# A four-block convolution kernel: strip semaphore, pointwise quarters, ScalarE's share and the last image's rows

## The reference

```python
x = x + _L0_conv_ref(_gn(x), W, pw, pb, cw, cb)          # kernels mixed per pixel
x = x + _L1_conv_ref(_gn(x), weights, tap_offsets)       # 9 taps at fractional offsets
x = x + _L2_conv_ref(_gn(x), gk1, gk2, w1, b1, ...)      # 4 gated experts, batch norm
x = x + _L3_conv_ref(_gn(x), w1, w2, alpha, bn...)       # two 3x3 convs, residual

# L0: para = conv3x3(relu(conv1x1(x, pw) + pb), cw) + cb            (16 coefficients per pixel)
#     t[o,e,p] = sum_j W[o,j,e] * patches3x3(x)[j,p];  out[o,p] = sum_e t[o,e,p] * para[e,p]
# L2, for each expert e: g = gate(x); y = relu(bn(conv3x3(g, w1[e]) + b1[e]))
#     out += relu(bn(conv3x3(y, w2[e]) + b2[e]) + x)
# L3: w1, w2 are sums of ten kernels weighted by alpha
#     out = relu(bn2(conv3x3(relu(bn1(conv3x3(x, w1))), w2)) + x)
```

## Time and profile before

| | us |
|---|---|
| median of 3 runs | 394.69 |
| lowest and highest | 394.27, 398.84 |
| profiled execution | 394.71 |
| its span | 392.8 |
| PE busy | 368.4 (94%) |
| DVE busy | 260.9 (66%) |
| POOL busy | 97.7 (25%) |
| ACT busy | 60.2 (15%) |

### The profile page before, as it was taken

The page is one execution under the profiler, slowest core; times in us unless marked ns, Lnnn a source line. Parts: engine busy times, 40 slices in busy tenths (PEclk is TensorE's granted clock), DMA queues, the critical chain, the costliest instruction groups (busy, mean ns, idle before and its releaser), DMA issues.

```text
span 392.8 us, 8970 instructions
## 1 busy us (share of the span) xinstructions
PE 368.4 (94%) x3446; PEld 261.1 (66%) x3446; DVE 260.9 (66%) x469; ACT 60.2 (15%) x129; POOL 97.7 (25%) x248
## 2 busy tenths in 40 slices
PE   4799999999999999999999999799999979799991
PEld 3557888888888888888888887323366742466670
DVE  4675777877878878878788788434425376902255
ACT  1125010010100100101001000420041029442200
POOL 4527777888600000000000000114010019400000
PEclk9999999999999999999999999889999989999998
DMA  7654847527357076173481000489600000000032
GB/s 225 167 138 121 202 119 194 153 53 199 98 127 200 23 187 160 47 199 101 117 204 26 0 0 0 105 183 217 126 2 3 2 1 2 0 3 5 3 108 110
DMA packets 28641, 38.59 MB, mean 98 GB/s; under 512 B 7072, under 2 KB 23776, under 8 KB 27936
## 3 DMA queue, kind: packets, MB, share of 16 engines
q1 hardware_dynamic: 18080, 27.52, 27.6%
q10 hardware_dynamic: 10528, 10.61, 10.4%
HBM read 4.56 MB, written 2.10 MB: 17 GB/s over the span
## 4 chain that ended last, share of the span: by engine, by line
PE 86%; DVE 7%; DMA 2%; ACTq 1%; issue 1%; ACT 1%; SPq 0%; POOL 0%; DVEq 0%; POOLq 0%
PE ps L866 23%; PE ps L867 23%; PE ps L870 8%; PE ps L917 8%; PE ps L1056 5%; PE ps L1040 5%; PE ps L901 4%; PE ps L985 3%; PE ps L1009 2%; DMA X<-in_x 2%; PE ps L841 2%; ACTq L374 1%; PE ps L1025 1%; PE ps L930 1%; PE ps L975 1%
## 5 line engine op out<-in xcount | busy, mean ns | idle before, releaser
L866 PE MATMUL ps<-WA,HS 128*128 128x512 f32 x384 | 153.6, 400 | 0.7 <-DVE TS L1121 0.7
L867 PE MATMUL ps<-WB,LS 128*128 128x512 f32 x384 | 150.7, 392 | 0.0
L1143 DVE TENSOR_TENSOR PROD<-ps,PT 128x512 f32<-128x512 f32 x128 | 88.4, 691 | 39.2 <-PE ps L870 33.4
L1127 DVE TENSOR_REDUCE RED<-PROD 128x32 f32<-128x512 f32 x128 | 86.4, 676 | 0.0
L866 PEld LDWEIGHTS ps<-WA,HS 128*128 128x128 f32 x384 | 72.4, 189 | 19.2 <-issue 0.9
L867 PEld LDWEIGHTS ps<-WB,LS 128*128 128x128 f32 x384 | 72.4, 189 | 14.9
L870 PE MATMUL ps<-WC,TS 96*128 96x512 f32 x128 | 50.6, 395 | 0.0
L482 POOL MEMSET IMG<- 128x67 f32 x1 | 0.2, 154 | 139.4 <-DVE X L1133 139.4
L901 PE MATMUL ps<-REPL,ONE 128*128 128x256 f32 x120 | 29.4, 398 | 1.7 <-DVE X L1328 1.3
L724 ACT ACTIVATE HS<-HS 32x40 fp32r<-32x40 f32 x21 | 5.7, 274 | 164.3 <-DMA TS<-LO 164.0
L917 PE MATMUL ps<-SK,WE 128*32 128x512 f32 x256 | 30.0, 628 | 0.0
(11 more groups left out here) (223 smaller groups left out, 335.0 us busy)
## 6 DMA issues: line engine op xcount, KB each, us to landing
LS<-HS SPq DMA_DIRECT2D x7, 960.0 KB, 5.8
HS<-HI SPq DMA_DIRECT2D x60, 80.0 KB, 2.5
SK<-IMG SPq DMA_DIRECT2D x32, 131.8 KB, 2.6
HS<-LO ACTq DMA_DIRECT2D x32, 80.0 KB, 2.7
LS<-LO ACTq DMA_DIRECT2D x32, 80.0 KB, 2.7
HS<-HI SPq DMA_DIRECT2D x30, 79.8 KB, 2.6
TS<-LO SPq DMA_DIRECT2D x34, 63.8 KB, 4.0
out_x<-OT SPq DMA_DIRECT2D x8, 256.0 KB, 2.1
```

What stands on the lines that cost most here:

```text
L866: pe.matmul(ps[b][:, :], px(HS, dy), WA[:, dy, :], start=(dy == 0), stop=False)
L867: pe.matmul(ps[b][:, :], px(LS, dy), WB[:, dy, :], start=False, stop=False)
L1127: ve.tensor_reduce(RED[j % 2][:, 32 * b:32 * b + 32], PROD[b % 2][:, :].rearrange("p (o e) -> p o e", e=E0), AX.X, ALU.add).then_inc(sum_d ...
L1143: ve.tensor_tensor(PROD[b % 2][:, :].rearrange("p (o e) -> p o e", e=E0), ps[b][:, :].rearrange("p (o e) -> p o e", e=E0), para.broadcast_ ...
```

## The change

- The eight DMAs of the first strip's lo rows signal a semaphore of their own, `first_lo`. VectorE waits for it after its first PT copy and clears the lo rows' column there; the wait for the remaining twelve DMAs and the clearing of TS stay behind the second copy. (The counts that later strips wait for are adapted.)
- The 1x1 convolution runs quarter 0 after three chunks and quarters 1 to 3 after all eight. One fill instead of two stands before the transposes.
- ScalarE writes hidden rows of images 1, 2 and 3, VectorE of image 0 and the constant rows; ten fills instead of thirteen.
- The sixteen raw z columns are copied by ScalarE, once VectorE has written the experts' means; ZE waits for them.
- The last image: VectorE writes rows 0 to 8 and then 9 to 14 of quarters 0 to 2; ScalarE rows 0 to 8 of quarter 3, row 15 of quarters 0 to 2, then rows 9 to 15 of quarter 3. The convolution's half h = 0 waits for the first parts and h = 1 for the last; two fills instead of four.

```diff
--- before.py
+++ after.py
@@ constants @@
-FIRST_REST = NREST - 5
+FIRST_REST = NREST - 13
-IMG_V = 40
...
+        def image_quarters(q0, q1, r0, r1):
+
+            return rows(IMG, 1, H).rearrange("p (q r) c -> p q r c", r=QR)[:, q0:q1, r0:r1, :]
+
+        def x_quarters(q0, q1, r0, r1):
+
+            return X[:, :].rearrange("p (q r c) -> p q r c", r=QR, c=W)[:, q0:q1, r0:r1, :]
...
-        def stack_lo(queue, s, half):
+        def stack_lo(queue, s, half, done):
...
-                                    LO[32 * b:32 * b + 32, :, bass.ds(s * (SL // 2) + g, S0)].bitcast(F32)).then_inc(strip_rest[half], 16)
+                                    LO[32 * b:32 * b + 32, :, bass.ds(s * (SL // 2) + g, S0)].bitcast(F32)).then_inc(done, 16)
...
@@ ScalarE @@
-            stack_lo(act, 0, 0)
+            stack_lo(act, 0, 0, first_lo)
...
-            for b in (1, 3):
+            for b in (1, 2, 3):
 
                 act.activation(hidden_rows(b, 1, 5), ps[b][:, 0:5 * W].rearrange("p (r c) -> p r c", c=W), ACT.Relu, bias=Q2[:, 7, 3:4],
                                scale=Q2[:, 7, 2:3]).then_inc(hidden_by_scalar, 1)
+            act.wait_ge(bn_input_ready, 2)
+            for e in range(NE):
+                for b in range(B):
+                    ins = act.activation(ZRAW[32 * e:32 * e + 32, b:b + 1], ps[e][32 * b:32 * b + 32, 6 * W + 1:6 * W + 2], ACT.Copy)
+                ins.then_inc(raw_z_done, 1)
             act.wait_ge(bn2_ready, 1)
...
             act.wait_ge(coef_ready, 3)
-            norm(rows(IMG, 1 + IMG_V, H - IMG_V), IMG_V, H).then_inc(image_by_scalar, 1)
+            for q0, q1, r0, r1 in ((3, 4, 0, CR + 1), (0, 3, QR - 1, QR), (3, 4, CR + 1, QR)):
+                act.activation(image_quarters(q0, q1, r0, r1), x_quarters(q0, q1, r0, r1), ACT.Identity, bias=NMR[:, 0:1],
+                               scale=RS[:, 0:1]).then_inc(image_by_scalar, 1)
             act.wait_ge(w3_mixed, 1)
-            act.wait_ge(image_by_vector, 3)
-            act.wait_ge(image_by_scalar, 3)
+            act.wait_ge(image_by_vector, 4)
+            act.wait_ge(image_by_scalar, 5)
             act.activation(X[:, :], X[:, :], ACT.Identity, bias=S3[:, 3:4]).then_inc(x3_shifted, 1)
...
@@ TensorE @@
-            for pair in range(2):
-                pe.wait_ge(norm0_done, 5 if pair == 0 else NCH)
-                tiles = [(b, j) for j in (2 * pair, 2 * pair + 1) for b in range(B)]
+            for chunks, quarters in ((3, (0,)), (NCH, (1, 2, 3))):
+                pe.wait_ge(norm0_done, chunks)
+                tiles = [(b, j) for j in quarters for b in range(B)]
...
-            fill_x(2)
+            fill_x(1)
...
-            fill(13)
-            pe.wait_ge(hidden_by_vector, 3)
-            pe.wait_ge(hidden_by_scalar, 2)
+            fill(10)
+            pe.wait_ge(hidden_by_vector, 2)
+            pe.wait_ge(hidden_by_scalar, 3)
...
             pe.wait_ge(coef_ready, 3)
-            fill(4)
+            fill(2)
             pe.wait_ge(w3_mixed, 1)
-            pe.wait_ge(image_by_vector, 3)
-            pe.wait_ge(image_by_scalar, 3)
             for h in range(2):
+                pe.wait_ge(image_by_vector, 3 + h)
+                pe.wait_ge(image_by_scalar, 4 + h)
                 for t in range(TAPS):
...
@@ VectorE @@
                 ve.tensor_copy(PT[:, 4 * j:4 * j + 4, :, :, :].rearrange("p u b h e -> p (u b h e)"), ps[4 + j][:, :]).then_inc(pt_by_vector, 1)
+                if j == 0:
+                    ve.wait_ge(first_lo, 16 * 8)
+                    ve.memset(wrapped(HS[0], slice(96, 128), 0).bitcast(F32), 0.0).then_inc(first_fixed, 1)
             ve.wait_ge(first_third, 4)
             ve.wait_ge(strip_rest[0], 16 * FIRST_REST)
-            ve.memset(wrapped(HS[0], slice(96, 128), 0).bitcast(F32), 0.0).then_inc(first_fixed, 1)
             ve.memset(wrapped(TS[0], slice(0, 96), W - 1).bitcast(F32), 0.0).then_inc(first_fixed, 1)
...
-            for b in (0, 2):
+            for b in (0,):
...
-            def raw_z(e):
-
-                for b in range(B):
-                    ve.tensor_copy(ZRAW[32 * e:32 * e + 32, b:b + 1], ps[e][32 * b:32 * b + 32, 6 * W + 1:6 * W + 2])
...
-            raw_z(0)
             ve.wait_ge(averaged, 1)
...
-            raw_z(1)
             ve.wait_ge(averaged, 2)
...
-            raw_z(2)
-            raw_z(3)
             ve.wait_ge(bn_power_done, 2)
...
+            ve.wait_ge(raw_z_done, NE)
             ve.tensor_scalar(ZE[:, :], ZRAW[:, :], QD[:, 0:1], QD[:, 1:2], ALU.mult, ALU.add).then_inc(z_by_expert, 1)
...
-            norm(rows(IMG, 1, IMG_V), 0, IMG_V).then_inc(image_by_vector, 1)
+            for r0, r1 in ((0, CR + 1), (CR + 1, QR - 1)):
+                ve.tensor_scalar(image_quarters(0, 3, r0, r1), x_quarters(0, 3, r0, r1), MV[:, 0:1], RS[:, 0:1],
+                                 ALU.subtract, ALU.mult).then_inc(image_by_vector, 1)
```

More of the change, by code:

```diff
@@ L241, in build @@
         first_third = sem("first_third")
+        first_lo = sem("first_lo")
         tile_done = sem("tile_done")
@@ L276, in build @@
         z_by_expert = sem("z_by_expert")
+        raw_z_done = sem("raw_z_done")
         experts_copied = sem("experts_copied")
@@ L726, in _ @@
             act.wait_ge(lo_done, 5)
-            stack_lo(act, 1, 1)
+            stack_lo(act, 1, 1, strip_rest[1])
             stack_third(act, 1, 1, (0, 1))
@@ L733, in _ @@
                     act.wait_ge(tile_done, (2 * it + half - 1) * B * STRIP_T)
-                    stack_lo(act, 2 * it + half, half)
+                    stack_lo(act, 2 * it + half, half, strip_rest[half])
                     stack_third(act, 2 * it + half, half, (0, 1))
@@ L1350, in _ @@
                         ve.tensor_copy(quarter_rows(q + 1, 2, 4, 0, 1), quarter_rows(q, 2, 4, QR, 1)).then_inc(halo_by_vector, 1)
-            ve.wait_ge(image_by_vector, 3)
-            ve.wait_ge(image_by_scalar, 3)
+            ve.wait_ge(image_by_vector, 4)
+            ve.wait_ge(image_by_scalar, 5)
             ve.wait_ge(x3_shifted, 1)
```

## The result

The changed kernel took 392.69 us (median of 17 runs, 389.57 to 394.19), the kernel before in the same comparison 396.41 (17 runs, 392.85 to 400.36). The ratio is 0.9921, with an interval of 0.9897 to 0.9945: a gain of some 3.1 us, inside two per cent. (The ratio leaves out executions over 1.5% above their kernel's fastest, three of the kernel before; so it gives less than the 3.7 us between the medians.) The profiled execution took 389.57 us with a span of 387.7, the fastest of its 17; the one of before, 394.71, lay under the 396.41 of this comparison. The two traces differ by 5.1 us, which is more than the change is worth, and the first thing to do is to say which part of that is clock.

A forecast was written before the change was run, and what follows sets the result against it. TensorE, holding 86% of the span, was taken as the bound. Direct gains of 1.0 + 0 + 0.7 + 0.25 + 0.7 = 2.65 us and 1.7 from the clock, off 394.7, gave 390.4 us; range 388.5 to 393.8.

The forecast's parts named there:

- the likeliest case: Whole kernel: direct gains of 2.65 us plus 1.7 from a shortened first half-clock stretch, giving 390.4 us; chance 0.40.
- the case in which both stretches stay: Half clock at the copies and at the experts unchanged, only direct gains count: 392.1 us; chance 0.28.
- the direct sum: Gains with the clock untouched, over all five parts of the change: 1.0 + 0 + 0.7 + 0.25 + 0.7 = 2.65 us.
- the clock's part: At the copies: work resumes before a clock fall fixed in program time, so 3.4 us less half clock, 1.7 gained.
- First tile: Main loop's first tile: starts at about 30.5 instead of 31.52, gain 1.0 us, bounds 0.7 to 1.2.
- the first tile doesn't move at all: Main loop's start: a late DMA binds instead of the transposes; 393.1 us, a variant without its own chance.
- The quarter ahead: Start, 1x1 convolution: TensorE ends earlier but ScalarE's ReLU waits behind six DMA issues; gain 0, bound 0.8 us.
- the rival: Before L841: 1.7 us idle instead of 0.68 makes the clock fall; 393.8 us, chance 0.10, or 395.5, chance 0.07.
- Hidden rows: Second masked convolution: starts at 300.3 instead of 301.00, gain 0.7 us, bounds 0.5 to 0.9.
- Raw z: Experts stage: sixteen copies moved to ScalarE, 3.2 us in all; gain 0.25 us, ZE 0.8 earlier but covered by half clock.
- The image: Last image's convolution: starts at 344.37 instead of about 345.1, gain 0.7 us, bounds 0.4 to 0.9.
- the price of half the stretch's length: TensorE at half clock costs half the stretch: 3.4 us at the copies, 1.7 at the experts, 5.1 together.

The follow-up runs named there:

- e1: The changed kernel run again without any edit: 391.35 us (4 runs), ratio 0.9883 to the kernel before.
- e12: Changed kernel plus dummy matmuls between the copies and after the averaging matmuls, ScalarE's stack DMAs waiting for the fourth instead of third chunk: 390.93 us, ratio 0.9885.
- e8: Changed kernel with VectorE's two image instructions each cut into three single quarters: 392.82 us in a single execution, only its stages read.
- e4: Changed kernel with the first strip's hi DMAs split nine on SP and three on ScalarE instead of six and six: 392.07 us (10 runs), ratio 0.9941.
- e9: Changed kernel with the three counts of dummy matmuls restored to 2, 13 and 4: 391.10 us in a single execution, only its stages read.
- e3: Changed kernel with the 1x1 convolution in two pairs of quarters again: 392.10 us (5 runs), ratio 0.9888.
- e6: Kernel before with dummy matmuls added between the copies and after the averaging matmuls: 395.81 us (12 runs), ratio 1.0031.
- e2: Kernel before with only the first tile's part of the change: 395.87 us (10 runs), ratio 0.9985.
- e10: Changed kernel with VectorE's first image part at ten rows a quarter, its second cut into single quarters: 395.23 us in a single execution, only stages read.

## Why the prediction was right, and where it wasn't

The forecast of a small gain and its range held. The gain was 3.1 us where the likeliest case had 4.35 (390.4), nearer to the case in which both stretches stay (2.65, 392.1). The kernel before took 396.4 in this comparison, not 394.7, but 394.7 less 3.1 lies inside the range as well. The chances, read as one list with the last 0.03 and 0.02, add up to 1.05. Of the likeliest case's two parts, the direct sum (2.65) stood up in the traces but hides one missed wait, and the clock's part (1.7) was wrong in its reason.

**First tile, 1.0 said, 0.97 in the profile shown, often less.** The step that failed is the cover of the new wait: "the last is issued at 26.54 and lands 2.3 us later". That was the median of a group of five; for the last one the trace of before gives no landing. The lo clearing waited for that DMA in eight of the twelve profiled executions that have the part, by 0.22 (e1) to 1.23 us (e12), which is one of the prediction's own signs of being wrong. This is e8's timeline:

```profile
26.46 0.69 ACTq L390 DMA_DIRECT2D LS<-LO  x1
...
31.02 0.09 DVE L1136 MEMSET HS<- 32x40 f32 x1 [1.06 <-DMA LS<-LO]
31.14 0.69 DVE L1133 COPY PT<-ps 128x512 f32<-128x512 f32 x1
31.37 0.47 PE L882 MATMUL ps<-WA,HS 128*128 128x512 f32 x1 [0.83 <-DVE HS L1136]
```

It landed about 4.5 us after its issue began, and the wait, placed ahead of the second PT copy, delays that copy too. How late it is issued decides: in the four executions without a wait its issue begins 4.25 to 4.73 us behind the second convolution, in the eight with one 5.21 to 5.79, because a DMA ahead of it in ScalarE's queue took up to 2.2 us to issue. Before it was 26.54 - 21.39 = 5.15, so the cover was thin from the start, and the 0.97 of the profile shown is partly luck. Over the ten profiled executions with this part and one fill (e4 and e9 left out) the distance is 9.14 to 10.27, in the mean 9.5, where the two executions with the old order have 10.13 and 10.12: the part is worth 0.6 us, and between nothing and 1.0 in a single execution. The case "the first tile doesn't move at all" was named, as a variant without a chance of its own; it is real.

**The quarter ahead, 0 said.** Right for executions in which ScalarE's issues take 5.0 us or more, as in both profiles the argument rests on. In others they take 4.4 and the part gains 0.3. The clock didn't fall ahead of the second convolution in any of ten executions; but this doesn't test the rival, because the longer idle time on which it rests didn't come. The prediction had 1.7 us in place of 0.68; it measured 0.76, and 0.29 to 1.07 in the ten. It overlooked that the fills themselves wait for VectorE (0.46 us, L1107) and so end at 20.4, not 19.7. Where the clock did fall at the start, it was earlier and with the pairs.

**Hidden rows, 0.7 said, 0.65.** By its own steps: three batches took 1.64 us (1.65 said), and the convolution began 1.78 us after the first. **Raw z, 0.25 said, 0.32**; sixteen copies in 2.80 us, 0.175 each (0.20 said, 3.2 in all; the measured time differs from the 1.6 us that the prediction estimated by the Trainium skill, ScalarE: Activation LUTs, What ACT_TABLE_LOAD costs, and the measurement decides), never last; ZE 0.8 us earlier as worked out, and worth 0.2 more where the clock is full. **The image, 0.7 said, 0.49.** Of the 0.2 that are missing nearly 0.1 is the start before, counted at 345.1 where TensorE began at 345.02. The mis-sized term is VectorE's first part, taken in proportion to the long instruction as 1.1 us; it measured 1.47: 275 ns and two thirds of the single rate, where half of it was assumed. ScalarE's two parts, 0.87 and 0.54, would have held the start nearly as long.

**The clock.** What was said, that the first stretch shortens because the copies come before a fall that keeps its place, fell with e1. The profile after even shows the shortening, and yet not for that reason: in e8 the copies resumed at 253.27, later than the 253.04 of before, and the stretch was 3.4 us too, and e3 had none at the copies but 6.8 us of it later, at 275. What makes a stretch long or short stays open. Two steps failed. One is the mechanism; the other the price of half the stretch's length, when TensorE runs ahead of the stack's DMAs. From 42.21 to 41.50 us the stage gave back 0.7 for 3.4 us less; in the mean of the six executions with 3.4 us (41.0) it is 1.2, against one with 6.8, and the last 3.4 us give nothing back (e6, 41.39). At the experts, where no DMA stands behind, the price is right for one stretch: the same changed kernel takes 7.35 with 3.4 us of it (e1) and 5.73 without, 1.6 us. It is too high for a long one: 10.2 us cost 3.6 (e2).

**What makes up the 3.1 us, then.** 0.6 to 1.0 of the first tile, 0.65, 0.32 and 0.49 are shown, 2.1 to 2.4 in sum. 0 to 0.3 of the quarter ahead and 0.2 where ZE counts are seen in single executions. The rest, up to 0.8, would be fewer half-clock stretches. The mean clock of the timed executions on record speaks for it (72 of the kernel before in the experiments' comparisons, two far outliers left out; 21 of the changed one). At equal mean clock the medians are 1.5 to 2.6 us apart: 394.95 (19 executions) and 392.86 (6) at 0.977 to 0.981, 395.22 (7) and 392.63 (7) at 0.985 to 0.987, 392.13 (11) and 390.60 (5) from 0.988 on. That is the size of the direct part. And 12 of the 21 stand at 0.985 or more, but only 18 of the 72. Which part of the change keeps the clock up, if one does, is not shown; at the start the pairs had half clock in two of four profiled executions.

## What to carry to other kernels

Dummy matmuls that keep the clock up are part of the path as soon as the work behind them gets faster: count them in when work is moved, and cut them with it (e9: all of the image's gain and two thirds of the hidden rows'). A DMA's landing time for a cover is that of the last one of a burst in several executions, not a median; and a wait that is moved forward in an in-order engine delays what stands behind it. Cut VectorE's tensor_scalar instructions from SBUF to SBUF so that the outermost count is even: three quarters, or odd rows of one, cost a third more or the double per column (e8, e10). Before putting a price on half clock, look for the DMA that TensorE would wait for at full clock; and compare single profiles by stages between events, not by spans.

## What the runs showed of the hardware

The half clock after short idle pieces didn't keep its place: the same kernel had it from 251.5 and not at the experts, then from 252.7 and from 314.1. Single profiled executions had from 0 (e12) to 17.1 us (e2) of it before the tail, in programs that differ little. One DMA instruction in ScalarE's queue took from 0.61 to 2.24 us to issue, six of them 4.4 or 5.0 to 5.6 us, from one execution to the next. And VectorE's tensor_scalar cost 0.52, 0.69 or 1.03 ns a column (on top of 275 ns) depending on how its rows are grouped.
